# Turning normalised tokens in 32x32 blocks on VectorE, with DMAs to place the blocks

## The reference

```python
def _L1_attn_ref(x, wq, bq, wk, bk, wv, bv, wo, bo, th1_w, th1_b, th2_w, th2_b):
    ...
    attn = jnp.einsum('bhnd,bhmd->bhnm', q, k) * scale
    attn = jnp.einsum('gh,bhnm->bgnm', th1_w, attn) + th1_b[None, :, None, None]
    attn = jax.nn.softmax(attn, axis=-1)
    attn = jnp.einsum('gh,bhnm->bgnm', th2_w, attn) + th2_b[None, :, None, None]
    out = jnp.einsum('bhnm,bhmd->bhnd', attn, v)
    ...
h = h + _L1_attn_ref(_layernorm(h, axis=-1), ...)
h = h + _L1_ffn_ref(_layernorm(h, axis=-1), ...)   # the mixture of experts: routes = argmax of a softmax
```

## Time and profile before

| | us |
|---|---|
| median of 3 runs | 4380.58 |
| the three runs | 4378.49 to 4381.98 |
| the profiled execution, its own time | 4380.37 |
| its span, first to last instruction | 4378.6 |
| first score of the phase to the last one's start | 1290.5 to 3654.9 |

### The profile page before, as it was taken

One profiled execution on the slowest core, in us unless ns is written; L12 is line 12 of the kernel. 1 busy time (PEld: TensorE's weight loads), 2 busy tenths in 40 slices (PEclk: granted clock), 3 DMA queues, 4 the chain that ended last, 5 costly groups with the idle time before them and its releaser, 6 DMA issues. The chain is left out here.

```text
span 4378.6 us, 201182 instructions
## 1 busy us (share of the span) xinstructions
PE 4176.6 (95%) x88202; PEld 3286.3 (75%) x88202; DVE 2534.3 (58%) x7273; ACT 2188.3 (50%) x5051; POOL 1717.9 (39%) x2794
## 2 busy tenths in 40 slices
PE   6998998999989999999999999999999999999998
PEld 4555665766657777777877877787778777999997
DVE  5776886666655655566565556555655554432332
ACT  3453443555536555555555555555555553213443
POOL 2223435776743333333333333333333331002565
PEclk8999999999999999999999999999999999999999
DMA  5112210000000000100000000000000001332333
GB/s 114 25 34 47 48 33 7 1 2 1 1 14 4 16 5 14 24 16 4 16 16 16 4 16 16 16 4 16 16 16 4 16 16 38 77 88 65 66 67 50
DMA packets 122908, 114.73 MB, mean 26 GB/s; under 512 B 64000, under 2 KB 110594, under 8 KB 122042
## 3 DMA queue, kind: packets, MB, share of 16 engines
q1 hardware_dynamic: 94646, 66.47, 6.5%
q0 software_dynamic: 16768, 23.59, 3.0%
q10 hardware_dynamic: 10628, 11.80, 1.2%
HBM read 59.89 MB, written 41.48 MB: 23 GB/s over the span
## 5 line engine op out<-in xcount | busy, mean ns | idle before, releaser
L2273 PE MATMUL PS<-th_kT,th_qg 64*61 64x274 f32 (+1 forms) x21120 | 1461.1, 393 | 9.4 <-issue 7.0
L1956 POOL TENSOR_TENSOR th_qg<-th_qT,w_th_th 128x180 f32<-128x180 f32 x1760 | 849.9, 505 | 1355.6 <-PE PS L2273 1344.3
L2152 ACT ACTIVATE th_P<-PS 119x600 f32<-119x600 f32 x880 | 649.6, 738 | 849.9 <-PE PS L2259 849.5
L2273 PEld LDWEIGHTS PS<-th_kT,th_qg 64*61 64x61 f32 (+1 forms) x21120 | 879.8, 132 | 204.5 <-issue 35.2
L2070 DVE TENSOR_REDUCE th_nmx<-PS 125x1 f32<-125x548 f32 x880 | 640.3, 728 | 632.5 <-PE PS L2273 632.0
L2259 PEld LDWEIGHTS PS<-th_mixn,th_P 61*55 61x55 f32 x35200 | 672.6, 125 | 173.4 <-issue 66.9
L2259 PE MATMUL PS<-th_mixn,th_P 61*55 61x60 f32 x35200 | 708.0, 214 | 48.3 <-issue 40.4
L2162 ACT ACTIVATE th_P<-PS,th_nb 125x548 f32<-125x548 f32 x880 | 623.1, 708 | 105.7 <-DVE th_nb L2073 105.5
L1388 POOL TENSOR_SCALAR ga_P<-ga_P,ga_rw 110x110 f32<-110x110 f32 (+4 forms) x240 | 264.9, 1115 | 160.5 <-DVE ga_rw L1556 159.7
L2073 DVE TENSOR_SCALAR th_nb<-th_nmx,w_th_b 125x1 f32<-125x1 f32 x880 | 240.2, 273 | 32.2
L2298 PE MATMUL PS<-th_P,th_v 119*32 119x90 f32 (+1 forms) x11520 | 250.4, 244 | 1.1 <-ACT th_P L2152 0.8
(11 more groups left out here) (369 smaller groups left out, 6291.8 us busy)
## 6 DMA issues: line engine op xcount, KB each, us to landing
pf_xT<-pf_spill SPq DMA_DIRECT2D x32, 412.5 KB, 5.5
ex_tokens<-th_xn SPq DMA_DIRECT2D x124, 82.5 KB
pf_spill<-pf_xT SPq DMA_DIRECT2D x16, 412.5 KB, 3.7
ex_turned<-th_rT SPq DMA_DIRECT2D x16, 412.5 KB, 3.7
ex_x<-ex_turned SPq DMA_DIRECT2D x32, 206.2 KB, 4.1
out_h<-X SPq DMA_DIRECT2D x16, 330.0 KB
ex_w<-in_L_ffn_W ACTq DMA_DIRECT2D x18, 288.0 KB
ex_w<-in_L_ffn_W ACTq DMA_DIRECT2D x8, 576.0 KB
```

What stands on the lines that cost most here:

```text
L1956: ins = pool.tensor_tensor(qg[:, m % SB, :, 64 * s:64 * s + HQ].rearrange("p c (h n) -> p c h n", n=QH), qT[:, im % 2, :, at + s * QH:at + ...
L2152: act.activation(P2[:, :, :, at * QT:(at + 1) * QT].rearrange("p t h (s n) -> p s (t h) n", s=2), PS[0:PK, MB:MB + 2, 0:VO].rearrange("p s ...
L2273: ins = pe.matmul(PS[o:w, bank + a, 0:HK], qg[s, p, c, o:w], kT[s, im % 2, c, :], start=c == 0, stop=c == NC - 1)
```

## The change

`xn` becomes 128 partitions high, with the padding rows set to 0 once. After normalising, VectorE transposes `xn` in place in blocks of 32x32 (`blocks_of`, two instructions: three tiles, then two). A block is then a turned block, but lies in the wrong place; `spread_blocks` moves the blocks into `xT` or `rT` with 24 DMAs per turn (four row blocks, two halves of the features, three column blocks each), issued by SP. TensorE's turn and ScalarE's copies stay only for the first norm of image 0 and for the second norm of image 15.

The first norm of an image moves from steps 0 to 11 of the image before it to steps 41 to 52 of the image two before it (the blocks at steps 53 and 54), GpSimd's power from step 5 to step 46. The second norm keeps its steps, with its blocks at steps 25 and 26. La moves from step 40 to step 44, next to Lb. The spare matmuls become 49, 47 and 25.

```diff
-    SPARE = (39, 43, 14)
+    SPARE = (49, 47, 25)
-             26: (("Q0", 1),), 31: (("Q1", 1),), 35: (("Q2", 1),), 40: (("K01", 1), ("La", -1)),
-             44: (("K2", 1), ("Lb", -1), ("V4", 1)), 54: (("V03", 1),)}
+             26: (("Q0", 1),), 31: (("Q1", 1),), 35: (("Q2", 1),), 40: (("K01", 1),),
+             44: (("K2", 1), ("La", -1), ("Lb", -1), ("V4", 1)), 54: (("V03", 1),)}
-        xn = sb("xn", [R, T, D])
+        xn = sb("xn", [128, T, D])
+        LAND = 16 * 4 * KC * (C // 32)
-            return [(part, b + d) for part, d in SLOTS.get(i, ()) if 0 <= b + d < B]
+            return [(part, b + d) for part, d in SLOTS.get(i, ())
+                    if 0 <= b + d < B and (part[0] != "X" or b + d == 0) and (part[0] != "R" or b + d == B - 1)]
+        def spread_blocks(eng, to, landed):
+            for q in range(4):
+                w = min(32, R - 32 * q)
+                for c in range(KC):
+                    for j in range(C // 32):
+                        at = c * C + 32 * j
+                        eng.dma_start(to[32 * j:32 * j + 32, c, 0:NP].rearrange("p (t n) -> p t n", t=T)[:, :, 32 * q:32 * q + w],
+                                      xn[32 * q:32 * q + 32, :, at:at + w]).then_inc(landed, 16)
 # SP
+                def next_turned(im):
+                    sp.wait_ge(x_blocks, 2 * im)
+                    if im > 1:
+                        sp.wait_ge(x_landed, LAND * (im - 1))
+                    sp.wait_ge(done["V"], count("V03", im - 1))
+                    spread_blocks(sp, xT, x_landed)
+                next_turned(1)
+                next_turned(2)
                 for im in range(B):
                     sp.wait_ge(rn_in, im + 1)
 ...
-                    sp.wait_ge(taken["R"], count("Rb", im))
+                    if im < B - 1:
+                        sp.wait_ge(r_blocks, 2 * (im + 1))
+                        if im:
+                            sp.wait_ge(done["L"], count("Lb", im - 1))
+                            sp.wait_ge(kept, 16 * im)
+                        spread_blocks(sp, rT, r_landed)
+                        sp.wait_ge(r_landed, LAND * (im + 1))
 ...
+                    if im + 3 < B:
+                        next_turned(im + 3)
 # GpSimd
+                pool.memset(xn[96:128], 0.0).then_inc(padded, 1)
-                    if i == 5 and 0 <= b < B - 1:
-                        pool.wait_ge(var, b + 2)
+                    if i == NTILE - 9 and b < B - 2:
+                        pool.wait_ge(var, b + 3)
 # VectorE
+                def blocks_of(t0, t1):
+                    tiles = xn[:, t0:t1, :].rearrange("p t d -> p (t d)")
+                    return dve.transpose(tiles, tiles)
 # next_norm, at its step 6 (step 47 of the image):
                         if im >= 3:
-                            dve.wait_ge(done["R"], count("Rb", im - 3))
-                            dve.wait_ge(saved, SAVE * (im - 2))
+                            dve.wait_ge(r_landed, LAND * (im - 2))
 ...
+                    if im and i in (12, 13):
+                        if i == 12:
+                            dve.wait_ge(xn_in, T * (im + 1))
+                        blocks_of(0 if i == 12 else 3, 3 if i == 12 else T).then_inc(x_blocks, 1)
 # last_norm, at step 15:
-                            dve.wait_ge(done["X"], count("Xa", im + 2))
+                            dve.wait_ge(x_landed, LAND * (im + 2))
 ...
+                    if im < B - 1 and i in (25, 26):
+                        if i == 25:
+                            dve.wait_ge(rn_in, im + 1)
+                            dve.wait_ge(saved, SAVE * (im + 1))
+                        blocks_of(0 if i == 25 else 3, 3 if i == 25 else T).then_inc(r_blocks, 1)
 ...
-                    if b + 1 < B:
-                        next_norm(b + 1, i)
+                    if b < 0:
+                        next_norm(0, i)
+                    if b + 2 < B:
+                        next_norm(b + 2, i - (NTILE - 14))
 # TensorE: Q0 to Q2
-                        pe.wait_ge(taken["X"], count("Xa", im))
+                        if im == 0:
+                            pe.wait_ge(taken["X"], count("Xa", 0))
+                        else:
+                            pe.wait_ge(x_landed, LAND * im)
 # TensorE: La and Lb
-                        pe.wait_ge(taken["R"], count("Rb", im))
+                        if im < B - 1:
+                            pe.wait_ge(r_landed, LAND * (im + 1))
+                        else:
+                            pe.wait_ge(taken["R"], count("Rb", im))
```

33 lines of the change are left out of this document (19 added, 14 removed).

## The result

The changed kernel took 4405.7 us (median of four runs, 4401.2 to 4410.0), the kernel before 4381.3 beside it: 1.0052 times as long, 95% interval 1.0040 to 1.0064. The forecast was 29 us less; it came out 24 us more. (The runs were made on several chips. The kernel before took 4359 to 4381 us on them, so kernels measured on different chips are set side by side as ratios to it.)

The account below looks back on a forecast made before the run. TensorE's instruction stream was taken to bound the kernel; transposes -40, logits -1, spares +3, start +7 and placing DMAs +2 sum to -29 us, from 4380.6 to 4351 us, range 4330 to 4375.

Parts of the forecast that it names:

- signs of being wrong: Issue idle up 20 us or more; mix-weight waits at steps 26, 27; normalisations, Q0 or La waiting for DMAs.
- The transposes, -40: Talking-heads phase: 300 of 320 TensorE transposes go, 0.133 us each, -40 us, all on the path.
- a microsecond taken from it is a microsecond of the span: Talking-heads phase: TensorE's instruction stream sets every step's time, so time taken from it shortens the span equally.
- Logits, -1: La and Lb both after K2: one operand-shape change fewer per image, 0 to -2.4 us, taken as -1.
- The moved first norm: Same VectorE work at steps 41 to 52, GpSimd's power at step 46; TensorE's wait moves too: 0 us.
- Instruction blocks, 0 with -15 to +15: TensorE's block ends shift by some tens of instructions within the steps: -15 to +15 us, taken as 0.
- Rival 1: Instruction blocks, each wanted earlier, eat the gain: +19 us and a few, 4374 us; chance 0.17.
- Spares +3: 168 more spare matmuls on TensorE at 0.0186 us each, keeping each image's instruction length: +3 us.
- vector turns: VectorE's four 32x32 transposes per image, 0.77 and 0.51 us, fill its waits for scores: 0 us.
- placing DMAs +2: 24 DMAs per turn on SP's queue, 14 us, hidden; their pieces share engines with instruction blocks: +2 us (0 to +8).
- start +7: Phase start: first score 4.2 us later behind image 1's first norm, slower clock 3 us: +7 us, 4 to 12.
- Rival 4: Placing DMAs don't overlap, VectorE then TensorE wait: slower than before, +260 us at 1.82 us per DMA; chance 0.05.

Follow-up runs that it names:

- e3: Kernel before without 300 of 320 TensorE transposes and their copies, with the changed kernel's spares, norms and logits unmoved: 4412.1 us, ratio 1.0123 to the kernel before.
- e13: e3 with useless products added in steps 13, 17 and 22 and 9 fewer spares an image: 4414.0 us, ratio 1.0116 to the kernel before.
- e6: Changed kernel with the first half of the logits (La) back at step 40, with its waits: 4382.9 us, ratio 1.0035 to the kernel before.
- e2: Changed kernel with first-norm statistics two steps earlier and second-norm statistics four steps earlier: 4359.2 us, ratio 0.9996 to the kernel before.
- e4: Changed kernel with one of the 24 placing DMAs per turn, the other 23 left out: 4383.5 us, ratio 1.0059 to the kernel before.
- e9: e7 with 32 more spares ahead of the second image, a shift of 1/2 block: 4324.1 us, ratio 0.9918 to the kernel before.
- e7: Changed kernel with the edits of e2 and e6 together, no shift of block ends: 4360.6 us, ratio 0.9979 to the kernel before.
- e14: e7 with 16 more spares ahead of the second image, a shift of 1/4 block: 4430.4 us, ratio 1.0157 to the kernel before.
- e15: e7 with 48 more spares ahead of the second image, a shift of 3/4 block: 4410.9 us, ratio 1.0097 to the kernel before.
- e10: e7 with 64 more spares ahead of the second image, a shift of one block: 4349.1 us, ratio 0.9978 to the kernel before.

## Why the prediction was wrong

Held against the steps of the working, in us for 15 images where nothing else is said. None of the signs of being wrong that the prediction named came: TensorE's issue idle, in the rows as in the earlier trace rows, rose by 16 us (48 to 64), not by 20, and no compute engine waited for a DMA. Of the signs of being right, the shorter images did not come. What failed stood mostly in terms put at nothing.

- **The transposes, -40: right as a term.** Their four steps lost 2.82 us an image, 42 us, and 48 when the stops in them are taken out. But the step "a microsecond taken from it is a microsecond of the span" failed, and with it the reading of the profile ahead of all sums: part of TensorE's instruction stream waits for its own code, and time taken out ahead of a block that has not landed comes back as a stop. e3 shows it bare (36 us less work, 50 us slower), e13 from the other side (91 us more work, no slower). That the stops are 40.4 us said how much was waited, not how close the other blocks were to being late.
- **Logits, -1: wrong.** Steps 40 and 44 grew by 1.16 us an image, 17 us, by the granted clock. I counted instructions and operand changes, not what twenty nine-column products at one step do to the clock, although the clock is in the windows. e6 took the growth back in the steps, and 12 us of it in the time.
- **The moved first norm, "what TensorE waits there moves too: 0": wrong.** In the kernel before, GpSimd waited 81.8 us in all for that variance (its trace, the waits) and steps 6 and 7 were 0.56 us longer than plain ones. Behind step 46 GpSimd waits 156 us, its products come in a row, and steps 47 and 48 grow by 1.04 us. Net 7 us. e2 took it back. Why VectorE's variance is later there than at step 5 was not tested; the length of step 44 is not needed for it, since in e6, where that is as before, VectorE's mix operation is stretched at step 47 in 12 images, and in 9 in the changed kernel.
- **The second norm "keeps its steps": priced at nothing, cost 14 us.** Its GpSimd power had stood behind the eight transposes of step 13, whose 1.05 us gave GpSimd and VectorE time. I named no work that hid it, and took its cover away. The traces show the cover: VectorE's mix operation at step 15 takes over 0.7 us in 1 image of the kernel before, in 15 of e3, where the transposes are gone and the norms are where they were, and in none of e13, where useless products stand at step 13 instead. e2 took this back too.
- **Instruction blocks, 0 with -15 to +15: the size is wrong.** Against the kernel before, the stops rose by 16 us in images 1 to 15 (23 in images 1 to 14, less in the last), beyond the bound; but the runs show what the bound should have been: one quarter of a block is worth up to 104 us. I sized it as a third of the idle there was, which bounds a loss by what is lost already. Rival 1 had the mechanism and the reason ("each block is wanted earlier") and priced it at +19, with a chance of 0.17. The Trainium skill (Runtime: NRT & Kernel Launch, Instruction fetch mechanics), weighed there, calls the crossing of a block's end mostly hidden; stops of 75 to 176 us in a phase of some 2,350 us say otherwise, and the measurement decides.
- **Spares +3, vector turns, placing DMAs +2, start +7: right, as far as the runs can tell.** The spares' group is busy 5 us longer (12.2 against 7.0), though the block that they shorten stops at step 1; 0.77 and 0.57 us for the turns against 0.77 and 0.51; 18.4 us for 24 DMAs, within 10 to 24, and what they cost beside that lies within the noise of e4; +5.0 at the start, 3.77 of idle time and 2.64 for the slower clock, less the 1.5 that Q and K took less. Rival 4 is out. VectorE's turns waited for nothing, the saves included.

The mean of images 1 to 14 grew by 1.27 us. By cause, with the stops taken out of the steps of the table: transposes -3.17, clock at step 44 +1.33, norms +1.63 (first 0.70, second 0.93), stops +1.65, all else -0.17. That is 18 us for the 14 images; image 0 is 6 us longer, image 15 is 10 us shorter, and the first mix is 6 us later, which makes the phase's last mix 19 us later and, with what follows, the span 20 us longer. The medians differ by 24.

The three causes undone together, at a good place of the block ends, give 0.9918. That it lies beside the 0.9932 that was forecast does not confirm the working: e9 holds three edits that the change did not have, still has 83 us of stops, and stands at the best of five places, where the kernel before was tried at two.

## What to carry to other kernels

Where "issue" stands inside groups of equal matmuls, look whether TensorE waits for its own instruction blocks. If it does, as here, work taken out of it can give nothing back or cost time (e3), and work put in can be free (e13); sweep the place of the block ends (spares of a few instructions, at quarters of a block) on both kernels before a change of 1% is called good or bad. When a step is removed, list who used its time as slack, also engines that the change does not touch, and when work of one kind is gathered in one place, look at the granted clock behind it.

## What the runs showed of the hardware

- A block of 256 instructions is ready 1.4 us after its packet has landed (all traces). Its packet of about 1.0 us starts 1.1 us after the last block end where TensorE does not stop, and 2.3 us after it ahead of the stops in dense steps (e3); two dense steps of 1.92 us leave no room for the second, and blocks of quick instructions that last under 3 us leave none for either. In e7, e14, e9, e15 and e10 the time is the same at shifts of no and of one block, with 2.4% between best and worst.
- The granted clock fell to its lower level with TensorE 100% busy (1716.20 to 1719.00), after twenty products of nine columns, in 11 of 16 images; with twelve of them four steps earlier it did not.
- VectorE's operations on SBUF took three to four times as long while GpSimd ran six products in a row (0.81 for 0.25 us, 1.54 for 0.44).
